# Feed-forward pieces of two layers issued in two halves, the first a half-step ahead

## The reference

```python
qkv = einsum('bnc,cd->bnd', x, w_qkv)                 # 16 heads of 8
q, k = rope(rmsnorm(q)), rope(rmsnorm(k))
attn = softmax(q @ k.T / sqrt(8))                     # 1024 x 1024 per head
x = layernorm(x + (attn @ v) @ w_proj + b_proj)
h = silu((x @ w1.T) * s1) * ((x @ w2.T) * s2)         # 128 -> 512
h = gelu((h @ h1.T) * sh1)                            # 512 -> 512
h = gelu((h @ h2.T) * sh2)                            # 512 -> 512
x = layernorm(x + (h @ w3.T) * s3)                    # 512 -> 128
```

## Time and profile before

| what | value |
|---|---|
| median of 3 runs | 390.14 us (388.29 to 392.93) |
| profiled execution | 389.85 us, span 388.1 us |
| mean granted TensorE clock | 0.976 |
| TensorE busy | 338.2 us, 87% |
| ScalarE busy | 306.1 us, 79% |
| VectorE busy | 202.5 us, 52% |
| POOL busy | 18.4 us, 5% |

### The profile page before, as it was taken

One profiled execution on the slowest core, in us unless ns is written; L12 is line 12 of the kernel. 1 busy time (PEld: TensorE's weight loads), 2 busy tenths in 40 slices (PEclk: granted clock), 3 DMA queues, 4 the chain that ended last, 5 costly groups with the idle time before them and its releaser, 6 DMA issues.

```text
span 388.1 us, 6219 instructions
## 1 busy us (share of the span) xinstructions
PE 338.2 (87%) x2093; PEld 136.5 (35%) x2098; DVE 202.5 (52%) x397; ACT 306.1 (79%) x347; POOL 18.4 (5%) x21
## 2 busy tenths in 40 slices
PE   8976488878799999998999989998999899969980
PEld 3533111111132244533322444433223535425750
DVE  1899927101145754354556634455477153665754
ACT  2566399999999989797999888889998987852430
POOL 2300000000010000001100000011000000021001
PEclk9999699999999999999999999999999999988997
DMA  7998933123033030020302300303031100000001
GB/s 246 345 375 276 380 128 96 32 66 98 5 93 93 6 98 0 19 79 2 123 29 68 96 0 0 96 0 125 0 96 52 45 0 0 0 27 0 0 2 32
DMA packets 16201, 31.33 MB, mean 81 GB/s; under 512 B 1522, under 2 KB 5106, under 8 KB 16178
## 3 DMA queue, kind: packets, MB, share of 16 engines
q1 hardware_dynamic: 15938, 30.23, 23.8%
q0 software_dynamic: 240, 0.79, 0.5%
HBM read 19.21 MB, written 9.44 MB: 74 GB/s over the span
## 4 chain that ended last, share of the span: by engine, by line
PE 60%; ACT 17%; DVE 12%; issue 9%; ACTq 0%; POOLq 0%; DVEq 0%; POOL 0%
PE ps L456 20%; ACT probs L718 16%; PE ps L503 14%; PE ps L443 10%; PE ps L493 4%; PE ps L584 4%; DVE ffn L898 2%; PE ps L537 2%; DVE probs L805 2%; DVE parts L794 2%; PE ps L632 1%; PE ps L616 1%; PE ps L416 1%; PE ps L473 1%; DVE x_lo L873 1%
## 5 line engine op out<-in xcount | busy, mean ns | idle before, releaser
L718 ACT ACTIVATE probs<-ps 128x1024 f32<-128x1024 f32 x256 | 241.3, 1051 | 29.8 <-PE ps L443 29.7
L456 PE MATMUL ps<-probs,va 128*9 128x512 f32 x1024 | 130.3, 598 | 14.3 <-ACT probs L718 12.7
L443 PE MATMUL ps<-qa,ka 32*128 32x512 f32 x512 | 74.5, 501 | 11.7 <-ACT probs L718 7.0
L443 PEld LDWEIGHTS ps<-qa,ka 32*128 32x128 f32 x512 | 29.9, 184 | 108.7 <-ACT probs L718 68.7
L898 DVE TENSOR_SCALAR ffn<-ps,col 128x512 f32<-128x512 f32 x36 | 27.0, 750 | 55.1 <-PE ps L503 50.9
L503 PE MATMUL ps<-g_hi,w_hi 128*128 128x512 f32 x108 | 45.4, 421 | 2.5 <-DVE ffn L898 2.5
L503 PE MATMUL ps<-g_lo,w_hi 128*128 128x512 f32 x108 | 42.4, 392 | 0.0
L456 PEld LDWEIGHTS ps<-probs,va 128*9 128x9 f32 x1024 | 17.8, 89 | 62.3 <-ACT probs L718 32.5
L835 DVE STREAM_TRANSPOSE o_tok<-ps 128x512 f32<-128x512 f32 x15 | 10.7, 716 | 44.8 <-PE ps L456 44.8
L503 PEld LDWEIGHTS ps<-g_hi,w_hi 128*128 128x128 f32 x108 | 20.2, 187 | 15.4 <-DVE ffn L898 4.3
L873 DVE TENSOR_TENSOR g_lo<-ffn,g_hi 128x512 fp32r<-128x512 f32 x36 | 24.9, 692 | 1.2
(11 more groups left out here) (103 smaller groups left out, 290.6 us busy)
## 6 DMA issues: line engine op xcount, KB each, us to landing
ka<-k_scr SPq DMA_DIRECT2D x16, 512.0 KB, 4.1
qa<-q_scr SPq DMA_DIRECT2D x16, 256.0 KB, 4.1
q_scr<-parts SPq DMA_DIRECT2D x6, 512.0 KB, 6.4
k_scr<-parts SPq DMA_DIRECT2D x6, 512.0 KB, 6.7
va<-v_all SPq DMA_DIRECT2D x16, 144.0 KB, 4.5
ffn<-in_h SPq DMA_DIRECT2D x2, 1024.0 KB, 8.7
xT<-in_x_t SPq DMA_DIRECT2D x4, 256.0 KB, 4.9
q_scr<-rope SPq DMA_DIRECT2D x2, 512.0 KB, 7.1
```

What stands on the lines that cost most here:

```text
L443: mm = pe.matmul(s_tile(u)[:, i, :], ka[rows, slot, kt * P:(kt + 1) * P], qa[rows, slot, :], start=True, stop=not shifted)
L456: mm = pe.matmul(ps[32 * h:32 * h + VW, O_BANK, :], va[:, g % 2, kt, h, :], probs[:, step % 4, h, :], start=(kt == 0), stop=(kt == KT - 1))
L718: nc.scalar.activation(probs[:, step % 4, 2 * pair:2 * pair + 2, :], s_tile(u), ACT.Exp).then_inc(exp_done, 1)
```

## The change

Each hidden piece (eight matmuls) is done in two calls of four. `hidden` gets an argument `half`: half 0 takes the bank by `mix` and does the input tiles k = 0 and 1, half 1 goes on in the same bank with k = 2 and 3 and signals `mix_ready`. Half 1 stays at the slots of `HIDDEN_SLOTS`. Half 0 is at the slot before (`HIDDEN_BEGUN`): 32, 35, 39, 41 and 43, 47, 50, 51. At a slot that both lists have (51), half 1 of the older piece comes first. `down` does its eight matmuls in one call as before. VectorE's and ScalarE's orders don't change.

```diff
+HIDDEN_BEGUN = tuple(tuple(slot - 1 for slot in slots) for slots in HIDDEN_SLOTS)
...
-            def from_tiles(bank, c, layer, w_of, first, passes):
+            def from_tiles(bank, c, layer, w_of, tiles, first, passes):
 
-                for k in range(HM):
+                for k in tiles:
                     if first:
                         pe.wait_ge(g_ready, 12 * c + HM * layer + k + 1)
                     todo = [(w, x) for w in w_at(w_of(k))[:1 + (passes > 2)] for x in (g_hi[:, k, :], g_lo[:, k, :])]
                     for i, (w, x) in enumerate(todo):
                         mm = pe.matmul(bank, w, x, start=(k == 0 and i == 0), stop=(k == HM - 1 and i == len(todo) - 1))
-                mm.then_inc(mix_ready, 1)
-
-            def hidden(base, c, layer, m, passes):
-                from_tiles(mix(base), c, layer, lambda k: (H1, H2)[layer] + k * HID + m * P, m == 0, passes)
+                if k == HM - 1:
+                    mm.then_inc(mix_ready, 1)
+
+            def hidden(base, c, layer, m, half, passes):
+                bank = ps[:, MIX_BANK, :] if half else mix(base)
+                from_tiles(bank, c, layer, lambda k: (H1, H2)[layer] + k * HID + m * P, range(2 * half, 2 * half + 2), m == 0, passes)
 
             def down(base, c, passes):
-                from_tiles(mix(base), c, 2, lambda k: W3 + k * P, True, passes)
+                from_tiles(mix(base), c, 2, lambda k: W3 + k * P, range(HM), True, passes)
...
                     if slot in HIDDEN_SLOTS[layer]:
-                        hidden(base, c, layer, HIDDEN_SLOTS[layer].index(slot), passes)
+                        hidden(base, c, layer, HIDDEN_SLOTS[layer].index(slot), 1, passes)
+                    if slot in HIDDEN_BEGUN[layer]:
+                        hidden(base, c, layer, HIDDEN_BEGUN[layer].index(slot), 0, passes)
```

## The result

The changed kernel takes 397.22 us (median of 6 runs, 396.30 to 398.15), the kernel before 389.60 (now 6 runs, 388.29 to 392.93; the 390.14 that the prediction started from was the median of the first 3). The ratio on record is 1.0157, 95% interval 1.0121 to 1.0194; the quotient of the two medians would be 1.0196, just outside it, so the change is worth 6.1 us by the ratio and 7.6 us by the medians. Predicted was 396.4, 6.3 us more than before. The profiled execution took 398.04, its span is 396.4.

What follows compares the result with a forecast made beforehand. TensorE and ScalarE were both taken as nearly full, with TensorE's order deciding when ScalarE gets logits. Three passes of 2.1 us added 6.3 to 389.85, giving 396.15, or 396.4 at the median; range 392.4 to 399.2 us.

Steps and rivals of the forecast that it cites:

- The price of a half: Four hidden matmuls on TensorE were priced at 1.11 us, from groups of two at 0.66 and eight at 2.04.
- The pause: Between hidden pieces, TensorE waits for the single mix bank's eviction: 1.23 us last matmul to next, 0.91 of it the turn.
- The step at slot 51: Second layer: two halves and the bank wait precede step 26's logits, 4.51 us after step 25's instead of 2.49.
- the walk: The prediction's tracing of TensorE's new order through one pass, with trace starts as clock: 396.4 us, chance 0.80.
- First layer, net 0: First hidden layer: old waits pay for four splits and the longer pause; net 0, bounds -0.70 and +1.2 us.
- the bound of -0.70: First layer's best case: the 0.70 us ScalarE idles before the fourth Gelu is won.
- Logits of step 25, +0.12: Second layer: the first two pieces' splits only rearrange, so these logits come 0.12 us late.
- No slack to step 28: From exp(26) to step 28's second logits pair, ScalarE's 2.14 us delay persists, less 0 to 0.05 of slack.
- The sum: Three passes of 2.1 us each add 6.3 us over the whole kernel.
- Rival (a): Matmuls behind an eviction go on at once, so the 0.91 us falls away: 393.6 us, or 391.7; chance 0.13.
- Rival (b): Faster: free splits win the waits at the fourth Gelu (0.70) and before exp(25) (1.50): 383.3 us; chance 0.03.
- Rival (c): Slower: new TensorE idle times drop the granted clock to 0.50 once a pass, giving 404.0 us; chance 0.04.

Runs made afterwards that it cites:

- e3: Kernel before, but TensorE waits for the bank of the second layer's fourth piece at slot 51, all eight matmuls still at slot 52: pass 80.94 us (before 80.03), ratio 1.0051.
- e2: Kernel before with only the second layer's fourth piece split, first half at slot 51: pass 82.05 us (before 80.03), ratio 1.0142.
- e5: Changed kernel with only the first layer's four pieces split, second layer whole: pass 80.16 us (before 80.03), ratio to before 0.9999.
- e7: Changed kernel with only pieces 1 to 3 of the first layer split: pass 79.42 us (before 80.03), ratio to before 0.9948.
- e8: Changed kernel with only the first layer's third piece split, first half at slot 39: pass 79.41 us (before 80.03), ratio to before 0.9920.
- e9: Changed kernel with only pieces 1 to 3 of the second layer split: pass 80.15 us (before 80.03), one run.
- e11: Changed kernel without the seven idle warm matmuls of step 28: lengths read 83.88 and 85.10 us (changed kernel 82.30), one run.
- e6: Changed kernel with the fourth pieces of both layers whole, other six split: pass 79.64 us (before 80.03), ratio to before 0.9914.

## Why the prediction was right

The sign and the mechanism held, and the time came within 0.8 us: 396.4 predicted, 397.22 measured. The change itself was forecast as 6.3 us; it is 6.8 by the passes, 6.1 by the ratio and 7.6 by the medians.

- The price of a half, 1.11: measured 1.11 to 1.13, and 0.98 for a step of values, 0.97 before. The reason given, that both rows lie on one line, says nothing, since any two do; what bears it out is that inside a group the matmuls start 0.23 us apart (163.70 and 163.93 in the trace of before).
- The pause: 1.23 from last matmul to next was predicted, 1.23 and 1.24 measured; e3 shows it alone.
- The step at slot 51: 4.51 predicted from logits to logits, 4.53 in after and 4.51 in e2. The wait before exp(26) is 2.59; the list of signs said about 2.7, but the walk itself makes it 0.55 + 2.02 = 2.57.
- First layer, net 0: its end came 0.14 late (150.90 in the times of before), just past the 150.8 that the prediction named as a sign against it, though its own walk ends at 150.81. The term was mis-sized by that 0.1, about what eight halves of 1.13 instead of 1.11 make; e5 gives 0.1 a pass. That old waits pay for the splits and the pause is right in sum. The walk did not say that piece 4's half alone costs 0.74 of it (e5 against e7) and that without it 0.6 would be won (e7, e8); that gain stood in the prediction only as the bound of -0.70.
- Logits of step 25, +0.12: they came 0.28 late, half of it brought along from the first layer, 0.12 to 0.14 from the second (e9).
- No slack to step 28: exp(26) 2.32 late, exp(27) 2.32, the second pair 178.21 - 2.22 - 173.68 = 2.31. Of the slack of 0 to 0.05 none is seen up to this pair; over the whole pass it is 0.05 (2.27).
- The sum: 3 x 2.27 = 6.8 instead of 6.3. The walk had 2.14 a pass (rounded down to 2.1, with 0.12 for the second layer's first pieces in it), so what is new is the first layer's 0.13. The medians are 7.6 apart; the further 0.8 lies within what the runs of before scatter (4.6).
- The rivals' times are not all on one base: 393.6, 383.3 and 404.0 count from the profiled execution, 0.3 below the base of the 396.4, while 391.7 is 0.2 more than 393.6 less 2.1 for the three Gelu waits. No chance hangs on it.

Rival (a), the pause that is none, is refuted by e3. Rival (b), faster, was right in one part: most of the 0.70 before the fourth Gelu can be won, and e8 wins about 0.6 of it, at the split that fills a wait of TensorE; the prediction had it only as a bound. Its other part, the 1.50 before the exps of step 25, stays in e8. Rival (c), the clock, did not come in the kernel after (1.00 in its passes). e11 shows that it can: with 2.94 us idle at the place that I named the clock fell.

The Trainium skill (TensorE: Matmul & The Clock Gate, section Loop structure matters more than you think) has the next tile's matmuls follow immediately while VectorE copies the last one out of PSUM. The traces here do not agree for a single bank, whose next use the program holds back until the eviction is done: e3 has 0.92 us idle there.

## What to carry to other kernels

Cutting blocks does not in general help two engines that wait for each other in turn. A half pays where it stands in a wait that its engine had (e8: one split, 0.6 us a pass), and costs all of itself where it stands ahead of what the other engine waits for (e2: 2.02 with its pause). With one bank, taking it early moves the wait for its eviction too, ahead of everything issued behind it; so check for each moved piece whether the piece before it ends right ahead of it. A sum near 0 can hide a gain and a loss: had the change left both fourth pieces whole, it would have been faster (e6). Walk the order with starts from the trace: this one gave the places compared above within 0.3 us.

## What the runs showed of the hardware

A group of 128x512 matmuls costs about 0.2 us beyond 0.23 for each: 0.66 for two (up), 1.11 to 1.13 for four, 2.04 for eight. The turn of the single bank, from the last matmul's start to the next one's with an eviction of 0.75 us between, is 1.23 to 1.24 us. TensorE's idle time of 1.31 us behind the seven unused matmuls left the granted clock at 1.00 (after); 2.94 us without them was followed by 1.2 GHz for some microseconds (e11), and the two lengths read grew by 1.6 and 2.8 us against after. The start of the loop differs by 4.4 us between kernels with the same source ahead of it.
